# A recommender tower on one core: blocks of 2, 4, 4, 4 and 2 tiles with 10 or 12 tables looked up, in place of four blocks with 11

## The reference

```python
combined = concat([dense[:, None, :], e], axis=1)            # 2048 x 27 x 128
inter = einsum('bfd,bgd->bfg', combined, combined)[:, iu, ju]  # 351 pairs
h = concat([dense, inter, dense], axis=1)                    # 2048 x 607
h = maximum(h @ W_top1 + b_top1, 0)                          # 512
h = maximum(h @ W_top2 + b_top2, 0)                          # 256
y = h @ W_top3                                               # 1
```

## Time and profile before

| what | value |
|---|---|
| median of three runs | 428.83 us |
| the profiled execution's own time | 430.39 us |
| its span, first to last instruction | 428.6 us |
| PE busy | 379.9 us (89%) |
| POOL busy | 258.4 us (60%) |
| DVE busy | 224.4 us (52%) |
| ACT busy | 145.6 us (34%) |
| granted TensorE clock, mean | 0.968 of full speed |

### The profile page before, as it was taken

One profiled execution on the slowest core, in us unless ns is written; L12 is line 12 of the kernel. 1 busy time (PEld: TensorE's weight loads), 2 busy tenths in 40 slices (PEclk: granted clock), 3 DMA queues, 4 the chain that ended last, 5 costly groups with the idle time before them and its releaser, 6 DMA issues.

```text
span 428.6 us, 7915 instructions
## 1 busy us (share of the span) xinstructions
PE 379.9 (89%) x3308; PEld 274.0 (64%) x3308; DVE 224.4 (52%) x414; ACT 145.6 (34%) x320; POOL 258.4 (60%) x248
## 2 busy tenths in 40 slices
PE   7738976359999979988999979989999979989997
PEld 7626855248566648878566648878466558879442
DVE  2927995005843539805944439806935349707300
ACT  2432743211322234442322234443222334442321
POOL 6888888760477777760477777760577777750000
PEclk9986989859999999999999999999999999999999
DMA  5992222210022132420122132320122232210000
GB/s 199 388 319 74 61 76 55 68 51 10 26 65 71 49 81 62 104 69 9 28 68 66 53 84 59 103 69 9 34 73 61 55 76 74 68 44 5 2 0 0
DMA packets 19872, 30.74 MB, mean 72 GB/s; under 512 B 5657, under 2 KB 13977, under 8 KB 19836
## 3 DMA queue, kind: packets, MB, share of 16 engines
q0 software_dynamic: 7680, 15.74, 14.3%
q1 hardware_dynamic: 12148, 14.48, 10.9%
q10 hardware_dynamic: 8, 0.01, 0.0%
HBM read 30.21 MB, written 0.01 MB: 70 GB/s over the span
## 4 chain that ended last, share of the span: by engine, by line
PE 67%; POOL 21%; issue 6%; DMA 3%; ACT 2%; POOLq 0%
POOL rows L340 21%; PE mix_ps L420 16%; PE emb_ps L363 11%; PE emb_ps L364 11%; PE mix_ps L393 8%; PE emb_ps L393 7%; PE mix_ps L431 6%; PE emb_ps L374 4%; DMA rows<-table,gather_ids 3%; PE mix_ps L439 2%; PE emb_ps L405 1%; ACT h L508 1%; ACT emb L469 1%; DMA gather_ids<-ids_gathered 0%; ACT emb L459 0%
## 5 line engine op out<-in xcount | busy, mean ns | idle before, releaser
L340 POOL DMA_INDIRECT rows<-table,gather_ids x240 | 257.4, 1073 | 123.3 <-issue 70.1
L536 DVE TENSOR_SCALAR hot<-lids,row_number 128x512 fp32r<-128x512 int16 x352 | 160.3, 504 | 91.1 <-PE emb_ps L364 80.4
L363 PE MATMUL emb_ps<-hot,table_hl 128*128 128x512 f32 x352 | 153.0, 435 | 10.6 <-DVE hot L536 10.6
L364 PE MATMUL emb_ps<-hot,table_hl 128*128 128x512 f32 x352 | 139.3, 396 | 0.0
L363 PEld LDWEIGHTS emb_ps<-hot,table_hl 128*128 128x128 f32 x352 | 67.4, 191 | 30.3 <-issue 14.6
L469 ACT ACTIVATE emb<-emb_ps 128x512 f32<-128x512 f32 x64 | 43.6, 687 | 109.6 <-PE emb_ps L374 108.4
L364 PEld LDWEIGHTS emb_ps<-hot,table_hl 128*128 128x128 f32 x352 | 67.4, 191 | 18.7 <-issue 6.3
L459 ACT ACTIVATE emb<-emb_ps 128x512 f32<-128x512 f32 x44 | 50.2, 1141 | 80.5 <-PE emb_ps L364 80.5
L374 PE MATMUL emb_ps<-ident,rows 128*128 128x128 f32 x256 | 40.6, 285 | 22.2 <-DMA rows<-table,gather_ids 22.2
L546 DVE STREAM_TRANSPOSE turned<-mix_ps 32x832 uint32<-32x832 uint32 (+1 forms) x24 | 25.2, 1049 | 63.8 <-PE mix_ps L393 63.4
L374 PEld LDWEIGHTS emb_ps<-ident,rows 128*128 128x128 f32 x256 | 31.7, 146 | 34.9 <-DMA rows<-table,gather_ids 25.5
(11 more groups left out here) (27 smaller groups left out, 106.6 us busy)
## 6 DMA issues: line engine op xcount, KB each, us to landing
lids<-ids_looked_up SPq DMA_DIRECT2D x44, 128.0 KB, 3.1
raw<-table SPq DMA_DIRECT2D x11, 512.0 KB, 10.2
rows<-table,gather_ids POOLq DMA_INDIRECT x240, 2.7
rows<-dense SPq DMA_DIRECT2D x16, 64.0 KB, 1.8
w_sb<-w_pairs SPq DMA_DIRECT2D x2, 256.0 KB
w_sb<-w SPq DMA_DIRECT2D x1, 512.0 KB
w_sb<-w_dense SPq DMA_DIRECT2D x1, 256.0 KB
w_stage<-w_dense SPq DMA_DIRECT2D x1, 256.0 KB
```

The source lines that it names most:

```text
L340: pool.indirect_dma_start(out=rows[:, use % ROW_SLOTS, q, :], out_offset=None, in_=tables[GATHERED[g]], in_offset=bass.IndirectOffsetOnAxi ...
L363: pe.matmul(bank[:, :], table_hl[:, i, 0, cols], hot[:, n % HOTS, :], start=(c == 0), stop=False)
L364: pe.matmul(bank[:, :], table_hl[:, i, 1, cols], hot[:, n % HOTS, :], start=False, stop=(c == CHUNKS - 1)).then_inc(hot_used, 1)
L536: dve.tensor_scalar(hot[:, n % HOTS, :], lids[:, k % LIDS, :], row_number[:, c:c + 1], None, ALU.is_equal).then_inc(hot_ready, 1)
```

## The change

The batch is cut into five blocks of 2, 4, 4, 4 and 2 tiles. They look up 10, 12, 12, 12 and 10 tables, so a tile has 16, 14 or 16 tables gathered (232 gathers in all, 240 before), in five groups in the tiles of the first and last block (17 vectors: 3, 3, 4, 3 and 4) and in four in the others (15 vectors: 3, 4, 4 and 4). Twelve tables are held in SBUF. A lookup of a block of two tiles is 256 columns wide. POOL's stop at the Gram tiles stays as it was.

Beside that: `hot` has seven places and `rows` six slots. The ids of block 0 come in one DMA that stands behind the second table (`first_lids`); those of later blocks are stored as three parts with a gap of one element behind each, and a one-hot is 513 columns wide (258 in the last block), with the surplus ids -1; `hots` reads three rows of 171 (or 86) elements and writes one run. The dense vectors are copied by ACT to a buffer of their own, `dense_x`, and `l1` with c = 3 reads that. `weights_load` is planned at 24 us, and `l3` is planned 9 us later.

```diff
-BLOCK_LOOKUPS = [11] * 4
+
+BLOCK_TILES = [2, 4, 4, 4, 2]
+BLOCK_LOOKUPS = [10, 12, 12, 12, 10]
...
+    FIRST_TILE = [sum(BLOCK_TILES[:b]) for b in range(BLOCKS + 1)]
+    BLOCK_OF = [b for b in range(BLOCKS) for _ in range(BLOCK_TILES[b])]
+    PLACE = [t - FIRST_TILE[BLOCK_OF[t]] for t in range(TILES)]
...
+    EMB_AT = [(BLOCK - wide) // 2 * PAIR_WIDE for wide in WIDE]
...
-    ROW_SLOTS = 8
+    ROW_SLOTS = 6
...
-    HOTS = 10
+    HOTS = 7
     LIDS = 3
+
+    PARTS = 3
+    PADDED = [wide if b == 0 else -(-wide // PARTS) * PARTS for b, wide in enumerate(WIDE)]
+    LID_AT = [sum(PADDED[:b]) for b in range(BLOCKS + 1)]
...
-    FIRST, LENGTH, GROUP_TIME = 98.0, 94.0, 5.0
+    LENGTH = [2.9 + 5.5 * 4 * n + 3.7 * n for n in BLOCK_TILES[:1]]
+    for b in range(1, BLOCKS):
+        LENGTH.append(5.1 * BLOCK_TILES[b - 1] + (0.93 * BLOCK_LOOKUPS[b] + 5.7) * BLOCK_TILES[b])
...
+    WEIGHTS_AT = 24.0
+    L3_LATER, EARLY = 9.0, 12.0
...
+    def last_rows(b):
+        return ends(b) - 3.7 * BLOCK_TILES[b] + 3.5
...
-            return 9.0 + 5.3 * (i + h / 2)
-        return begins(b) + 4.8 + 5.8 * (i + h / 2)
+            return 9.0 + (5.3 if BLOCK_TILES[0] == 4 else 3.6) * (i + h / 2)
+        return begins(b) + 4.8 + (last_rows(b) - begins(b) - EARLY) / BLOCK_LOOKUPS[b] * (i + h / 2)
 
     def embed_time(t, e):
-        g = GROUP_NO[t, e] - GROUP_NO[t // IN_BLOCK * IN_BLOCK, 0]
-        return begins(t // IN_BLOCK) + GROUP_TIME * (g + 1) + 2.9
+        b = BLOCK_OF[t]
+        groups = BLOCK_TILES[b] * len(GROUP[t])
+        g = GROUP_NO[t, e] - GROUP_NO[FIRST_TILE[b], 0]
+        return last_rows(b) - (groups - 1 - g) * (last_rows(b) - begins(b) - 7.9) / (groups - 1)
...
-    at(-5, "weights_load")
+    at(-18.5, "first_lids")
+    at(WEIGHTS_AT, "weights_load")
     for k in range(len(LOOKS)):
-        at(look_time(k - LIDS, 1) + 2.0 if k >= LIDS else -30 + k, "lids", k)
+        if LOOKS[k][0] > 0:
+            at(look_time(k - LIDS, 1) + 2.0, "lids", k)
...
+        rows_at, first = last_rows(b), FIRST_TILE[b]
+        for j in range(BLOCK_TILES[b]):
+            t = first + j
+            at(rows_at - 3.0 if j == 0 else rows_at + 0.5 + 3.6 * (j - 1), "gram", t)
+            at(rows_at + 0.4 if j == 0 else rows_at + 0.5 + 3.6 * j + 0.1, "turn", t)
+            at(rows_at + 0.5 + 3.6 * (j + 1) + 0.2, "pairs", t)
         after = ends(b)
         at(after + 0.1, "l1", b, 3)
         for c in range(3):
-            at(after + 5.0 + 0.1 * c, "z", b, c)
-            at(after + 6.5 + 4.0 * c, "l1", b, c)
+            at(after + 5.5 + 0.1 * c, "z", b, c)
+            at(after + 6.5 + (0.5 + 0.9 * BLOCK_TILES[b]) * c, "l1", b, c)
+        part = BLOCK_TILES[b] / 4
         for n in range(N1):
-            at(after + 16.0 + 1.0 * n, "h1", b, n)
-            at(after + 18.6 + 1.8 * n, "l2", b, n)
-        at(after + 25.5, "h2", b)
-        at(after + 27.0, "l3", b)
-    at(58, "weights")
+            at(after + 7.0 + (9.0 + 1.0 * n) * part, "h1", b, n)
+            at(after + 7.6 + (11.0 + 1.8 * n) * part, "l2", b, n)
+        at(after + 8.0 + 17.5 * part, "h2", b)
+        at(after + 8.0 + 17.5 * part + L3_LATER, "l3", b)
+    at(WEIGHTS_AT + 12.0, "weights")
...
+        first_lids = nc.alloc_sbuf_tensor_at("first_lids", [128, BLOCK_LOOKUPS[0], WIDE[0]], i16, offset=room_at)
...
-        hot = sb("hot", [128, HOTS, BLOCK], fp32r)
-        lids = sb("lids", [128, LIDS, BLOCK], i16)
+        hot = sb("hot", [128, HOTS, max(PADDED) + 1], fp32r)
+        PART_WIDE = -(-BLOCK // PARTS) + 1
+        lids = sb("lids", [128, LIDS, PARTS, PART_WIDE], i16)
+        dense_x = sb("dense_x", [128, BLOCK])
...
-        dense_part = bass.AP(emb, FEATURES - 1, [[EMB_WIDE, 128], [32 * PAIR_WIDE, BLOCK // 64], [SECOND, 2], [PAIR_WIDE, 32]])
...
+            def load_first_lids():
+
+                sp.dma_start(first_lids[:, :, :], bass.AP(ids_looked_up.tensor, 0, [[0, 128], [ids_looked_up.shape[1], BLOCK_LOOKUPS[0]], [1, WIDE[0]]])) \
+                    .then_inc(first_lids_in, 16)
+
             def load_lids(k):
-                wait(sp, hot_ready, CHUNKS * (k - LIDS + 1))
+                if k - LIDS >= BLOCK_LOOKUPS[0]:
+                    sp.wait_ge(hot_ready, CHUNKS * (k - LIDS + 1))
                 b, i = LOOKS[k]
-                sp.dma_start(lids[:, k % LIDS, :],
-                             ids_looked_up[i:i + 1, b * BLOCK:(b + 1) * BLOCK].to_broadcast([128, BLOCK])) \
+                sp.dma_start(lids[:, k % LIDS, :, 0:PADDED[b] // PARTS],
+                             ids_looked_up[i:i + 1, LID_AT[b]:LID_AT[b + 1]].to_broadcast([128, PADDED[b]])) \
                     .then_inc(lids_in[k % LIDS], 16)
...
-                if t % IN_BLOCK == 0:
+                if PLACE[t] == 0:
...
-                    x = dense_part
+                    x = dense_x[:, 0:WIDE[b]]
...
-                    wait(act, dense_used, t // IN_BLOCK)
-                at_pair = t % IN_BLOCK * 64 * PAIR_WIDE
+                    wait(act, dense_used, BLOCK_OF[t])
+                    act.activation(by_turn(dense_x[:, PLACE[t] * TILE:PLACE[t] * TILE + TILE]),
+                                   by_number(bank[:, 128 * n - 128:128 * n]), ACT.Copy)
+                at_pair = EMB_AT[BLOCK_OF[t]] + PLACE[t] * 64 * PAIR_WIDE
...
-                if h == 0:
-                    dve.wait_ge(lids_in[k % LIDS], 16 * (k // LIDS + 1))
+                if h == 0 and k < BLOCK_LOOKUPS[0]:
+                    dve.wait_ge(first_lids_in, 16)
+                elif h == 0:
+                    dve.wait_ge(lids_in[k % LIDS], 16 * len(range(k, BLOCK_LOOKUPS[0] - 1, -LIDS)))
+                b, i = LOOKS[k]
+                wide = PADDED[b]
+                ids = first_lids[:, i, :] if b == 0 else lids[:, k % LIDS, :, 0:wide // PARTS]
                 for c in range(h * CHUNKS // 2, (h + 1) * CHUNKS // 2):
                     n = k * CHUNKS + c
                     wait(dve, hot_used, n - HOTS + 1)
-                    dve.tensor_scalar(hot[:, n % HOTS, :], lids[:, k % LIDS, :],
+                    dve.tensor_scalar(hot[:, n % HOTS, 0:wide], ids,
                                       row_number[:, c:c + 1], None, ALU.is_equal).then_inc(hot_ready, 1)
...
+    ends = np.cumsum(BLOCK_TILES) * 128
+    low_ids = np.concatenate([low_ids[:, :ends[0]]] + [np.pad(low_ids[:, a:b], ((0, 0), (0, -(b - a) % 3)), constant_values=-1)
+                                                       for a, b in zip(ends[:-1], ends[1:])], axis=1)
```

## The result

In ten runs of each kernel, taken in turn, the changed kernel took 427.05 us (425.04 to 428.03) and the kernel before 429.26 (427.92 to 431.49). The ratio is 0.9944, with a 95% interval of 0.9921 to 0.9966: faster, by 0.6%, where 417.0 was forecast. The range holds the time, but the gain is a fifth of the one forecast. The profiled execution took 427.44 us with a span of 425.6, 3.0 less than before, at a mean granted clock of 0.988. The experiments further down ran on three other chips, on which the kernel before took 501.3, 435.2 and 432.1 us; on the first of these the kernel before was 17% slower and transfers came late, so its four runs were repeated.

The account below looks back on a forecast made before the run. PE and POOL were taken as tied bounds of the later blocks. Block 0 62.3 + block 1 87.6 + 2 x 95.6 + block 4 57.6 + tail 18.2 = 416.9 us of span; forecast 417, range 405 to 428.

Parts of the forecast that it names:

- DVE's sum for block 1: Block 1: DVE done 66.2 us after block 0's Gram phase, below POOL's 68.8; the block costs 87.6.
- Block 0: First block, 2 tiles: ends at 62.3 us, bounds 56 to 66; DVE done near 43.7, POOL last.
- rival C: Short one-hots let block 0's gathers through, Gram starting at 46.3, and one-hots cost 0.60 us: 407 us, chance 0.20.
- G0: End of block 0's Gram phase, forecast at 62.3 us.
- Blocks 2 and 3: Middle blocks: 95.6 us each; PE 74.5 of work, full ring leaves 41 one-hots missing after l3, a 2.2 us wait.
- The price of a one-hot: Blocks 1 to 4: a gapped one-hot of 513 columns costs DVE 0.635 us, chosen between 0.60 and 0.66.
- Block 4 and tail: Last block of 2 tiles costs 57.6 us, PE 48.0 plus Gram phase 9.6; the tail after it 18.2.
- Rival E: Half-wide lookups are bound by their weight loads, 0.191 us a matmul, 10.6 in block 4: 428 or 431 us, chance 0.10.
- D: The ids' new form changes nothing: one-hots stay at 0.394 us, gathers at 1.32; 415 us in all, chance 0.08.
- What the profile was to show: Gathers at 1.25, one-hot near 0.72 long, PE waiting for `hot` late in blocks 2 and 3, rows late ending block 1.
- Rival B: One-hots are dearer and DVE becomes the bound; slower than before from 0.72 us each, 436 us at 0.757; chance 0.10.
- three signs of being wrong: Gathers still taking 1.3 us, one-hots over 0.7, or PE's matmul of 256 columns over 0.15.

Follow-up runs that it names:

- one-part run: The changed kernel with the ids of blocks 1 to 4 in one run, without gaps: 418.81 us, ratio 0.9617 to the kernel before.

## Why the prediction was wrong in size

The step that failed is DVE's sum for block 1, which left out that a full ring stops DVE: 66.2 us where 75.6 were measured. Beside it the one-hot was priced at 0.635 us and cost 0.656.

**Block 0: the number held, its route did not.** I had POOL slowed to 1.75 us and ending last. The 26 gathers of the window above took 1.25 each, and POOL had done all 32 by 43.5. DVE ended last instead, at 49.83, for a forecast 43.7: the ids, 640 KB in one DMA, took 11.8 us to land and one-hots began at 13.9 for 10.9, and while POOL works a short one-hot takes 0.32 us from start to start, not 0.26. From DVE's timeline:
```profile
26.22 2.64 DVE L580 TENSOR_SCALAR hot<-first_lids,row_number 128x256 fp32r<-128x256 int16 x8
28.78 1.27 DVE L566 TENSOR_TENSOR table_hl<-raw,table_hl 128x1024 fp32r<-128x1024 f32 x1
...
45.46 2.18 DVE L580 TENSOR_SCALAR hot<-first_lids,row_number 128x256 fp32r<-128x256 int16 x8
47.56 1.22 DVE L566 TENSOR_TENSOR table_hl<-raw,table_hl 128x1024 fp32r<-128x1024 f32 x1
```
Eight of them take 2.56 us up to the table's rest in the first pair of rows, 2.10 in the second, when POOL has stopped. The DMA engines fall quiet at that time too, but they don't explain it: the four one-hots from 41.25 to 42.55 still took 0.32 each with POOL at work and a DMA share of 0.16.
Gram began at 51.16, which is to the tenth what the forecast's terms give (47.2 + 2.86 + 1.1). That is luck: a POOL that was too slow in the sum stood in for a DVE that was too quick. The 1.6 us by which the block was shorter lie in the Gram phase, put at 5.6 us for its first tile at the lower clock. From the chain of waits:
```profile
51.16 3.93 PE mix_ps L430 x128
```
The granted clock was 1.00 there and in the 7.6 us ahead, in which PE was busy for 5.87; before the change it was 0.66 in that tile, behind 7.9 us with PE busy for 2.14.
So rival C's condition, gathers let through, came true, but its 46.3 for the start of Gram did not, for the two reasons above. Its other condition, one-hots at 0.60, was false.

**Block 1: the step that failed.** I wrote DVE as 3.25 + 61.0 + 0.5 + 1.35 = 66.2 (it is 66.1) and POOL as last at 68.8. Gram began 75.6 after G0: 3.2 of turn, 96 x 0.656 = 63.0, the 7.0 of a full ring, 0.4 because the last one-hot of each run takes its full 0.74, and 2.0 to Gram. That sum has 2.0 us from the dearer one-hot and 7.0 that I left out: I let DVE run as if nothing held it back, and counted the ring in blocks 2 and 3 only. But a block with a network in it, of two tiles or four, stops DVE at the start, and DVE is late at the end. Of the 9.4 us by which DVE was later than forecast 2.6 lie under POOL's 68.8. The Gram phase gave 1.7 back (17.05 for 18.8): the first Gram tile was not at the lower clock (granted 1.00, 3.94 us), from the chain of waits:
```profile
136.31 3.94 PE mix_ps L430 x128
...
153.36 1.06 DVE turned L590
```

**Blocks 2 and 3: the mechanism right, its size off.** l3, from the chain of waits:
```profile
201.60 1.81 PE mix_ps L476 x4
```
It was over 203.41 - 153.36 = 50.05 us in, as forecast. In the 9.2 us since DVE's last restart 14 one-hots had been made, so 57 - 14 = 43 were missing, for 41. With 0.656 in place of 0.635 that makes 2 x 0.656 + 41 x 0.021 = 2.2 of the 2.4 by which Gram began later; the Gram phase was 0.7 shorter.

**The price of a one-hot**, 0.656, lies at the 0.66 which I had as one element a cycle with today's fixed cost; I chose 0.635 for the sum of weights' sake, an operation of another kind. The rows of this kernel give both: 513 elements in 0.656 and 258 in 0.40 (block 4) make 1.0 ns an element and 0.13 fixed for a one-hot, where 512 in 0.60 and 1024 in 1.14 make 1.05 and 0.07 for the sums. So the fixed part goes with the operation, not with the engine. The Trainium skill's rule ("VectorE: DVE Perf Modes", What auto-detection actually checks), two elements a cycle only for outermost dimensions that are even or equal, agrees with all forms run here: 512 to 512 at 0.40 (the one-part run too), three rows to 513 at 0.656, 256 to 256 at 0.26 with POOL at rest.

**Block 4 and tail.** Rival E is out: from start to start 256 columns take 0.12 (395.98 to 396.10 in the chain), so the weight loads don't bind. In the tail, l1's 24 matmuls take 5.86 for 5.2, 0.244 each for 0.217, as I had halved their time with the columns and kept no fixed part. In block 4 the fill took 1.0 more than forecast; PE waited 1.2 us there for h_x, but I have not redone the whole sum. D is out too, since the ids' form changed both prices. The one-part run is what D describes for the middle blocks, and it took 418.8, on another chip, for D's 415.

**What the profile was to show**: gathers at 1.25, yes; DVE's one-hot near 0.72 long, 0.74; PE waiting for `hot` in the last third, yes, though only on the weight loads; rows late at the end of block 1, no, one-hots were. **Rival B**, one-hots as the bound, is in mechanism what happened, without its price: I let it in from 0.66 on only because I had set the ring's stops in block 1 at nothing. With the 7.0 us added, DVE is last in block 1 from p = (68.8 - 12.2) / 96 = 0.59 up. Its dearest price, 0.757, comes out at 0.77 by its own words, which changes nothing here. None of the three signs of being wrong appeared (gathers at 1.3, one-hots over 0.7 from start to start, a matmul of 256 columns over 0.15): they watched prices, and what failed was a wait.

## What to carry to other kernels

A bounded ring between two engines turns a pause of the consumer that outlasts the free places into lost time of the producer. If the producer is the later bound, sum its time from its last restart, with all that is still missing, and not from the average: an engine at 74% busy can set the end. Work of the consumer counts before that restart and not behind it: l3 ahead of it cost 7.3 us, the strided operand 7.0, and spreading the same work with nothing taken away gained 7.2. Before giving one engine's time for another's, look in which stretches each is last: the gaps gained in the one block where POOL was, and lost in the others.

## What the runs showed of the hardware that I had not expected

The trade between DVE and POOL goes either way. With one-hots of 512 columns in block 0 gathers were slowed to 1.5 to 2.0 us at 0.40 a one-hot. With 256 columns gathers kept their 1.25 us and the one-hots paid, 0.32 for 0.26. In the blocks of the one-part run gathers took 1.32 beside one-hots at 0.41. The Trainium skill says ("SBUF — State Buffer", Who interferes with whom) that the two-port form locks out the other engine for the whole instruction and that whoever issues first has it; the runs agree in that gathers beside gapped one-hots keep their 1.25. That the ports are the reason is the page's; no run here shows it. Who pays in which case no run here settles.

The chip itself can matter more than the change: on the first one the kernel before was 17% slower (501.3 for 429.3), and three of the four kernels beside it stood on the other side of it than on the later chips. The two with fewer DMA packets were the quicker ones, 487 us with 21350 packets and 501 with 19872 (the kernel before); the three with more took 508 with 33125, 519 with 31136 and 520 with 32164, not in the order of their packets. The gapped ids make up the difference, since they come in three pieces. That the packets are the reason was not tried.
